# Two-layer perceiver block on one core: the mask of the first key block moves from matmuls on the identity into a stacked row, and two tables of step numbers change

## The reference, cut to what matters

```python
def xattn(query, key, value, mask, ...):        # x (2,256,256), ctx (2,4096,256), 16 heads of 16
    q = split(query @ w_q.T + b_q); k = split(key @ w_k.T + b_k); v = split(value @ w_v.T + b_v)
    scores = where(mask, -inf, (q @ k.T) / 4)   # mask (1,1,256,4096): True hides a key
    return softmax(scores) @ v  -> @ w_o.T + b_o
x = x + xattn(layernorm(x), ctx, ctx, mask, ...)
x = x + retention(layernorm(x), ...)            # 4 heads, rope, decay, gate
x = x + experts(layernorm(x), ...)              # 8 experts, gates below 0.1 dropped
```

## Time and profile before

| | us |
|---|---|
| median of 3 runs | 245.83 (245.18 to 247.62) |
| the profiled execution's own time | 246.22 |
| its span in the trace | 244.3 |
| PE busy in the span | 223.3 (91%) |
| DVE busy | 151.4 (62%) |
| ACT busy | 111.5 (46%) |
| POOL busy | 42.5 (17%) |
| mean granted PE clock | 0.988 |

### The profile page before, as it was taken

How to read it: one execution, slowest core, us unless ns; L and a number is a source line. 1 busy time by engine, 2 the same in 40 slices (tenths; PEclk the granted TensorE clock), 3 DMA queues, 4 the chain that set the end, 5 groups by cost and what they waited for, 6 DMA issues and landing times.

```text
span 244.3 us, 3831 instructions
## 1 busy us (share of the span) xinstructions
PE 223.3 (91%) x1394; PEld 122.9 (50%) x1394; DVE 151.4 (62%) x349; ACT 111.5 (46%) x237; POOL 42.5 (17%) x45
## 2 busy tenths in 40 slices
PE   8699999799799999999999898989898988899892
PEld 8368554444455645454544434535745753635340
DVE  3493789937626559696865073494457538586682
ACT  2245845557157476767677684233053051201000
POOL 6003999959000400000000000000000000000000
PEclk9999999999799999999999999999999999999997
DMA  6589678037409500550000000000000000000000
GB/s 189 198 213 321 198 183 332 4 78 179 102 13 262 163 1 3 170 179 1 3 2 3 1 0 0 1 3 0 0 0 3 0 1 1 0 0 24 23 25 25
DMA packets 15233, 17.74 MB, mean 73 GB/s; under 512 B 2573, under 2 KB 14313, under 8 KB 15209
## 3 DMA queue, kind: packets, MB, share of 16 engines
q1 hardware_dynamic: 13929, 17.11, 24.1%
q10 hardware_dynamic: 1280, 0.33, 0.7%
HBM read 9.79 MB, written 0.52 MB: 42 GB/s over the span
## 4 chain that ended last, share of the span: by engine, by line
PE 60%; DVE 18%; DMA 7%; SPq 6%; ACT 4%; issue 3%; DVEq 0%; ACTq 0%
PE bank L811 9%; PE bank L795 8%; PE bank L996 8%; PE bank L733 6%; DVE cneg L1561 6%; DMA ctxT<-in_ctxT 6%; PE bank L903 6%; PE bank L694 4%; SPq L399 4%; PE bank L976 3%; PE bank L864 3%; PE bank L681 3%; ACT prob L1245 2%; SPq L390 2%; PE bank L884 1%
## 5 line engine op out<-in xcount | busy, mean ns | idle before, releaser
L1561 DVE TENSOR_REDUCE cneg<-bank 128x1 f32<-128x896 f32 x64 | 68.0, 1087 | 32.7 <-PE bank L733 32.6
L1245 ACT ACTIVATE prob<-bank 128x512 f32<-128x512 f32 x112 | 65.5, 597 | 28.0 <-PE bank L795 19.3
L795 PE MATMUL bank<-qstack,kstack 99*128 99x256 bf16 x224 | 42.3, 274 | 1.3 <-ACT prob L1245 1.1
L733 PE MATMUL bank<-kstack,qstack 96*128 96x448 bf16 x128 | 38.5, 354 | 2.8 <-DVE cneg L1561 2.8
L811 PE MATMUL bank<-prob,vals 128*32 128x256 f32 x448 | 35.8, 391 | 0.4 <-ACT prob L1245 0.4
L795 PEld LDWEIGHTS bank<-qstack,kstack 99*128 99x128 bf16 x224 | 17.4, 97 | 24.8 <-issue 10.8
L903 PE MATMUL bank<-w_late,xnT 128*128 128x512 f32 x48 | 22.0, 595 | 0.3 <-ACT xnT L1274 0.3
L733 PEld LDWEIGHTS bank<-kstack,qstack 96*128 96x128 bf16 x128 | 12.4, 98 | 12.0 <-DVE cneg L1561 4.0
L996 PE MATMUL bank<-ctxT,xnT 128*128 128x512 f32 x32 | 17.1, 616 | 0.3 <-DVE x_in L1742 0.3
L1742 DVE SCALAR_TENSOR_TENSOR x_in<-bank,nwts,x_in 128x256 f32<-128x256 f32 x32 | 15.5, 484 | 2.5 <-PE bank L996 1.4
L996 PE MATMUL bank<-kpart,xnT 128*128 128x512 f32 x32 | 16.3, 592 | 0.0
(11 more groups left out here) (148 smaller groups left out, 277.9 us busy)
## 6 DMA issues: line engine op xcount, KB each, us to landing
kstack<-kpart SPq DMA_DIRECT2D x24, 224.0 KB, 3.6
w_late<-in_w_ret SPq DMA_DIRECT2D x1, 1536.0 KB
mask_all<-in_mask SPq DMA_DIRECT2D x2, 512.0 KB, 5.0
ctxT<-in_w_exp SPq DMA_DIRECT2D x1, 1024.0 KB
kpart<-in_w_exp SPq DMA_DIRECT2D x1, 1024.0 KB
ctxT<-in_ctxT SPq DMA_DIRECT2D x2, 448.0 KB, 6.6
ctxT<-in_ctxT SPq DMA_DIRECT2D x1, 896.0 KB, 8.8
qstack<-acc SPq DMA_DIRECT2D x12, 64.0 KB, 3.7
```

What stands on the lines that cost most here:

```text
L733: mm = pe.matmul(out, qstack[0:MROW, h, b, qt * P:(qt + 1) * P], kstack[0:MROW, b, h, half_ * HC:(half_ + 1) * HC], start=True, stop=not h ...
L795: mm = pe.matmul(out[:, hh * NQ:(hh + 1) * NQ], kstack[0:KROWS, b, h, kt * P:(kt + 1) * P], qstack[0:KROWS, h, b, :], start=(hh == 0 or no ...
L1245: act.activation(prob[:, n % PROBS, :], bank[:, S0 + jj, :], ACT.Exp).then_inc(c["prob_ready"], 1)
L1561: dve.tensor_reduce(cneg[:, st % 2, i:i + 1], bank[:, pair:pair + 2, 0:HC], AXXY, ALU.max, negate=True).then_inc(c["max_read"], 1)
```

## The change

- The mask of the first block becomes one more row of the stacks: row 96 of `kstack` holds -1e30 for hidden keys of the first block and 0 elsewhere, row 96 of `qstack` ones, and the three parts of the maximum move to rows 97 to 99. The maximum tiles contract 97 rows (before 96), the scores 100 (before 99). The matmuls L738 and L799 are gone from the fast branch.
- The rows of ones on the key side come by DMA from a small tile `edge` (4 x 896: zeros, then three rows of ones), at the end of each `stack_keys`; for n = 0 POOL fills them by a memset of 4 x 3584, and ACT issues a DMA with the mask row after making it (`first_row`). The three later memsets on POOL are gone. Ones on the query side are memset once: batch 0 by DVE at the very start, batch 1 by POOL ahead of `queries_cut(1)`.
- ACT counts per key of the first block how many queries hide it (`count_hidden`); DVE and the existing sum turn the fast branch off if any count is neither 0 nor 256.
- Stage 1's tiles go to steps `(m - 10) * 2 // 3`: steps 0 to 3 hold tiles 10, 11 / 12 / 13, 14 / 15 (before 10, 11 / 12, 13 / 14, 15 / none). So the rows of stage 1 are turned at step 5 (before 4).
- `LATER`: the keys n = 3 go to step 8 (before 5), the first values of batch 1 to step 12 (before 11).
- SP stacks the second batch right after the branch; the rows of stage 1 come after the keys n = 2, and the late weights after them.

```diff
@@ -47,7 +48,7 @@
-KROWS = MROW + 3
+KROWS = MROW + 4
@@ -83,7 +85,7 @@
         elif st == 1:
-            out.append((m - FIRST_TILES) // 2)
+            out.append((m - FIRST_TILES) * 2 // 3)
         else:
@@ -97,7 +99,7 @@
-LATER = {5: ("k", 3), 11: ("v", 0), 18: ("v", 1)}
+LATER = {8: ("k", 3), 12: ("v", 0), 18: ("v", 1)}
@@ -175,6 +178,10 @@
+    def stacked(self, n):
+        return self.at(f"k_stacked{n}", 96 if self.loop else 96 + 16)
@@ -252,8 +259,11 @@
-        hide_q0 = sb("hide_q0", [P, QT, P], BF16)
-        hide_k0 = sb("hide_k0", [P, NQ], BF16)
+        hides0 = sb("hides0", [P, NQ], BF16)
+        hidden_from = sb("hidden_from", [P, 1])
+        edge = sb("edge", [KROWS - MROW, CH], BF16)
@@ -388,6 +398,11 @@
+            def stack_edges(n, loaded):
+                b, f = divmod(n, KIN)
+                sp.dma_start(kstack[MROW:KROWS, b, f * HF:(f + 1) * HF, :], edge[:, :].unsqueeze(1).to_broadcast([KROWS - MROW, HF, CH])
+                             ).then_inc(loaded, 16)
@@ -436,6 +451,7 @@
             stack_keys(only, 1)
+            stack_edges(1, only["k_stacked1"])
             fast = is_fast(sp)
@@ -443,19 +459,21 @@
             with sp.If(fast > 0):
-                late_weights()
-                load_rows(only, 1)
                 stack_second_batch()
                 stack_keys(only, 2)
+                load_rows(only, 1)
+                stack_edges(2, only["k_stacked2"])
+                late_weights()
                 load_rows(only, 2)
                 stack_keys(only, 3)
+                stack_edges(3, only["k_stacked3"])
                 late_constants()
@@ -499,15 +521,12 @@
-            def rows_of_ones(n):
-                b, f = divmod(n, KIN)
-                rows = kstack[MROW:KROWS, b, f * HF:(f + 1) * HF, :].rearrange("r h k -> r (h k)").bitcast(F32)
-                pool.memset(rows, TWO_ONES).then_inc(s["ones_ready"], 1)
-                pool.wait_ge(s["ones_ready"], n + 1)
-            pool.wait_ge(s["const_ready"], 2)
-            rows_of_ones(0)
+            pool.memset(edge[:, :], 1.0).then_inc(s["edge_ready"], 1)
+            pool.wait_ge(s["edge_ready"], 1)
+            pool.memset(edge[0:1, :], 0.0).then_inc(s["edge_ready"], 1)
+            pool.wait_ge(s["edge_ready"], 2)
+            pool.memset(kstack[MROW:KROWS, 0, 0:HF, :].rearrange("r h k -> r (h k)").bitcast(F32), TWO_ONES).then_inc(s["ones_ready"], 1)
+            pool.wait_ge(s["ones_ready"], 1)
@@ -555,6 +574,9 @@
+            in_rows = qstack[MROW:KROWS, :, 1, :].bitcast(F32)
+            pool.memset(in_rows, TWO_ONES).then_inc(s["ones_ready"], 1)
+            pool.wait_ge(s["ones_ready"], 2)
             queries_cut(1)
@@ -592,20 +614,15 @@
                 pool.wait_ge(s["q_cut"], 3)
-                pool.wait_ge(*only.at("max_cut", 1))
-                rows_of_ones(1)
                 keys_cut(only, 2)
-                pool.wait_ge(*only.key("k_cut", 2))
-                rows_of_ones(2)
                 keys_cut(only, 3)
-                pool.wait_ge(*only.key("k_cut", 3))
-                rows_of_ones(3)
                 stream_and_bias()
@@ -714,28 +731,27 @@
                     pe.wait_ge(q_stacked[2 * b + g // 2], 96)
-                    pe.wait_ge(*c.at(f"k_stacked{2 * b + g // 2}", 96))
+                    pe.wait_ge(*c.stacked(2 * b + g // 2))
                     if c.loop:
                         settle(pe)
+                if b and g == 0 and not c.loop:
+                    pe.wait_ge(s["ones_ready"], 2)
                 if m == 0:
-                    pe.wait_ge(s["ident_ready"], 16 + 1)
                     pe.wait_ge(s["q0_taken"], 1)
...
                     else:
-                        pe.wait_ge(s["hide_first"], 2)
+                        pe.wait_ge(s["ones_ready"], 1)
+                        pe.wait_ge(s["rows_of_one"], 2)
                 pair = take_pair(c, "m", m)
...
                     out = bank[:, pair + half_, 0:HC]
-                    hides = c.loop or half_ == 0
-                    mm = pe.matmul(out, qstack[0:MROW, h, b, qt * P:(qt + 1) * P], kstack[0:MROW, b, h, half_ * HC:(half_ + 1) * HC],
-                                   start=True, stop=not hides, skip_group_check=True)
+                    mm = pe.matmul(out, qstack[0:MROW + 1, h, b, qt * P:(qt + 1) * P], kstack[0:MROW + 1, b, h, half_ * HC:(half_ + 1) * HC],
+                                   start=True, stop=not c.loop, skip_group_check=True)
                     if c.loop:
                         mm = pe.matmul(out, identb[:, :], hide_q[:, qt, half_ * HC:(half_ + 1) * HC], start=False, stop=True, skip_group_check=True)
-                    elif half_ == 0:
-                        pe.matmul(out[:, 0:P], identb[:, :], hide_q0[:, qt, :], start=False, stop=True, skip_group_check=True)
                 mm.then_inc(c["max_ready"], 1)
@@ -789,14 +806,12 @@
-                hides = c.loop or kt == 0
...
-                                   start=(hh == 0 or not hides), stop=not hides, skip_group_check=True)
-                if hides:
-                    hidden = hide_k[:, kt, :] if c.loop else hide_k0[:, :]
-                    mm = pe.matmul(out, identb[:, :], hidden.unsqueeze(1).to_broadcast([P, 2, NQ]),
+                                   start=(hh == 0 or not c.loop), stop=not c.loop, skip_group_check=True)
+                if c.loop:
+                    mm = pe.matmul(out, identb[:, :], hide_k[:, kt, :].unsqueeze(1).to_broadcast([P, 2, NQ]),
@@ -1153,10 +1169,18 @@
-            def hide_first():
+            def first_row():
...
-                act.activation(hide_k0[:, :], mask_k0[:, :], ACT.Copy, scale=HIDDEN).then_inc(s["hide_first"], 1)
+                act.wait_ge(s["edge_ready"], 2)
+                act.activation(edge[0:1, 0:P], mask_q0[0:1, 0, :], ACT.Copy, scale=HIDDEN).then_inc(s["first_row"], 1)
+                act.wait_ge(s["first_row"], 1)
+                act.wait_ge(s["ones_ready"], 1)
+                act.dma_start(kstack[MROW:MROW + 1, 0, 0:HF, :], edge[0:1, :].unsqueeze(1).to_broadcast([1, HF, CH])).then_inc(only["k_stacked0"], 16)
+            def count_hidden():
+                act.activation(hides0[:, :], mask_k0[:, :], ACT.Copy, accum_out=hidden_from[:, :]).then_inc(s["first_row"], 1)
@@ -1469,6 +1494,9 @@
+            dve.memset(mpart[:, :, :, 0, :], 1.0).then_inc(s["rows_of_one"], 1)
+            dve.memset(qstack[MROW:KROWS, :, 0, :].bitcast(F32), TWO_ONES).then_inc(s["rows_of_one"], 1)
@@ -1070,7 +1084,8 @@
-                pe.matmul(bank[0:1, OB, ODD_ALL:ODD_ALL + 2], minus[:, :], early_sums[:, :], start=True, stop=True,
+                pe.wait_ge(s["uneven"], 1)
+                pe.matmul(bank[0:1, OB, ODD_ALL:ODD_SUMS], minus[:, :], early_sums[:, :], start=True, stop=True,
```

More of the change, by code:

```diff
@@ L341, in build @@
         mask_loaded = [sem(f"mask_loaded{t}") for t in range(QT)]
-        only = Chunk({n: sem(n) for n in [*PER, *("first_k_" + n for n in ("hi", "taken", "mid", "cut"))]}, 0, False)
+        only = Chunk({n: sem(n) for n in [*(n for n in PER if n not in LOOP_ONLY), *("first_k_" + n for n in ("hi", "taken", "mid", "cut"))]}, 0, False)
         loop_sems = {n: sem(f"loop_{n}") for n in PER}
@@ L466, in _ @@
                 sp.wait_ge(s["more_ready"], 2)
+                sp.wait_ge(s["windows_added"], 1)
+                sp.wait_ge(s["edge_cleared"], 1)
+                for n in range(NB * KIN):
+                    stack_edges(n, s["edges_again"])
                 count = sp.value_load(n_windows[0:1, 0:1], min_val=1, max_val=NCH)
@@ L605, in _ @@
                 pool.wait_ge(s["q_cut"], 3)
-                rows_of_ones(1)
-                rows_of_ones(2)
-                rows_of_ones(3)
+                pool.wait_ge(*only.stacked(0))
+                pool.wait_ge(*only.stacked(1))
+                pool.memset(edge[0:1, :], 0.0).then_inc(s["edge_cleared"], 1)
+                pool.wait_ge(s["edge_cleared"], 1)
                 pool.wait_ge(s["more_ready"], 2)
@@ L1379, in _ @@
             act.wait_ge(s["odd_summed"], 1)
-            act.activation(odd_row[:, 0:ODD_ALL + 2], bank[0:1, OB, 0:ODD_ALL + 2], ACT.Copy, accum_out=any_odd[:, :]).then_inc(s["odd_counted"], 1)
+            act.activation(odd_row[:, 0:ODD_SUMS], bank[0:1, OB, 0:ODD_SUMS], ACT.Copy, accum_out=any_odd[:, :]).then_inc(s["odd_counted"], 1)
             act.wait_ge(s["odd_counted"], 1)
@@ L1495, in _ @@
             first_layernorm(1)
+            dve.wait_ge(s["first_row"], 2)
+            dve.scalar_tensor_tensor(early_sums[:, 2:3], hidden_from[:, :], float(NQ), hidden_from[:, :], ALU.subtract, ALU.mult).then_inc(s["uneven"], 1)
             def start_again():
@@ L1506, in start_again @@
                 for n in range(KIN):
-                    dve.wait_ge(*only.at(f"k_stacked{n}", 96))
+                    dve.wait_ge(*only.stacked(n))
                 for n in range(NB * KIN):
```

37 lines of the change are left out of this document (20 added, 17 removed).

## The result

| | before | after |
|---|---|---|
| median of the runs (lowest to highest) | 246.23 us (245.18 to 247.62), 4 runs | 239.97 us (239.15 to 240.14), 4 runs |
| profiled execution, span | 246.22, 244.3 | 239.15, 237.2 |
| mean granted clock in it | 0.988 | 0.995 |

The changed kernel takes 0.9736 of the time, 95% interval 0.9685 to 0.9788: 6.3 us less, 240.0 where 240.3 was forecast. A second comparison gave 0.9828 (0.9777 to 0.9879; 241.06 and 245.56). The two intervals overlap only from 0.9777 to 0.9788; what differs between them is shown further on, with the clock.

What follows compares the result with a forecast made beforehand. PE, busy 91%, was taken as the bound, with DVE setting the pace in the early steps. Terms 0 + 0 + 0.2 + 4.5 gave 4.7 with the clock's fall, 6.3 without; forecast 240.3 us, range 237.9 to 243.3.

Steps and rivals of the forecast that it cites:

- The price of the masks: Steps of kt = 0 and tiles on PE: 0.06 per query mask, 0.22 per key mask, start to start.
- Start: Up to 38.55, before step 1: the added memsets, small activation and DMA are hidden by waits; 0 us.
- the cover: Start, on POOL: the added memset of 1.8 fits into its idle 2.25 before the scan, 0.4 left.
- Steps 0 to 8: From 38.55 to step 9: 0 us, DVE sets the pace and a 1.2 wait for stage 1's rows eats the rest.
- Steps 9 to 12: Gain 0.2: masks 0.3, wait -0.1 (1.65 for DVE at tile 26, was 1.54), and the clock at half chance.
- Step 13 to the end: PE stays the bound: gain 4.5, between 3.8 and 4.8, from tile masks 2.2, key masks 2.2 and 0.4, less 0.3.
- the clock's fall: Steps 9 to 12, whether the clock falls again: half chance each; total gain 4.7 with it, 6.3 without.
- All waits go: Rival: stage 1's rows land in time, the key cut hurts at most 0.4, no clock fall: 237.1; chance 0.10.
- The early waits grow: Rival: stage 1's rows land late behind key stacks, clock falls behind both waits: 243.3, up to 244.5; chance 0.19.
- The 97th row: Rival: a fourth group of 32 rows makes each tile matmul 0.06 longer: 247.0; chance 0.03.
- the general branch: Rival: the first block's mask is judged uneven, the branch with loops runs, far above the time before; chance 0.02.

Runs made afterwards that it cites:

- masks_off: The kernel before without its two kinds of mask matmuls, memsets and order kept: 240.78 us, ratio 0.9774.
- old_order: The changed kernel with the order of before (last keys step 5, late values step 11, two tiles per early step), run twice: 238.86 and 237.69 us.
- memsets_first: The kernel before with POOL's three late memsets of ones moved to the start: 247.36 us, ratio 1.0012.
- cut_after: The changed kernel, POOL's cut of the last keys waiting until DVE has cut the maxima of stage 2: 238.75 us, ratio 0.9691.
- all_three: The changed kernel, POOL's last key cut and bias sum held behind DVE's cuts of stages 2 and 3, stage 1's rows turned a step sooner: 237.76 us, ratio 0.9701.
- after_again: The changed kernel unaltered, timed once more in the second comparison: 241.06 us, ratio 0.9828.

## Why the prediction came out right

**The price of the masks: right.** 0.06 and 0.22, start to start. Each later stage is 12.12 - 11.25 = 0.87 shorter, forecast 8 x 0.06 + 2 x 0.22 = 0.92, and masks_off without any new order or edge has the same pitch.

**Start: the cover held.** Tile 0 and step 1 come 0.8 and 0.7 earlier. Tile 0 follows the first keys on PE, and these the first context transfer: 7.94 before, 6.54 after, 7.74 to 7.76 with tile 0 at 22.70 and 22.73 in the two runs of old_order, which has the same start as the changed kernel. So the 0.8 is mostly when that transfer landed. The ten profiles with the new edges have tile 0 between 21.86 and 22.73, the three of the old kernel with its memset in place 22.90, 24.00 and 24.30 (the last two with the clock down at the start); whether the change has a share in that stays open. One reading of mine was wrong: POOL's memset of ones is not longer (3.08 for four rows, as for three before), but it starts at 3.39 instead of 1.73, behind the two memsets of `edge`. So it runs until 6.47 and held a TENSOR_SCALAR of the first layer norm for 1.32 instead of 0.17, which I had not counted; the keys on PE covered it. memsets_first shows what becomes of it without the cover.

**Steps 0 to 8: right.** Forecast 0, measured 19.21 before and 18.85 after from step 1 to step 9. DVE's reads set the pace, and the rows of stage 1 cost 1.01 for 1.2.

**Steps 9 to 12: the mechanism right.** DVE's CAST and subtraction took 0.96 and 0.90, and PE waited 1.41 for 1.65 before tile 26; cut_after took the cause away and the wait with it. I gave the clock half a chance to fall; in the profiled execution it did not, and 13.96 became 11.48, a gain of 2.5 where the sum had 1.8 for that case.

**Step 13 to the end: the term that failed.** I had 4.5, between 3.8 and 4.8; measured are 76.94 - 73.48 = 3.5. The step was "only the tile two behind a cut comes within 0.1, for which I take off 0.3 in all": it looked at DVE and PE alone. I had asked what a faster PE makes collide for the keys, not for POOL's sum of the bias, which starts when SP's queue has let its row through. It now meets the cut of stage 3 and costs 0.8 at tile 34 (all_three: 15.16 to 14.33 between two turns). The remaining 0.2, and the 0.3 that I had already taken off, went in small pieces that no run takes apart (a later stage gained 0.87 for 0.92).

**The total** of the profiled execution, 7.1, is my 6.3 without the clock's fall, plus 0.7 at the start, plus 0.4 and 0.7 in the steps 0 to 8 and 9 to 12, less 1.0 from step 13 on. That 240.3 was hit to 0.3 is partly such cancelling.

**The clock explains most of why two comparisons differ.** Each run has its mean granted clock and span. The kernel before at 0.996, five runs: 241.5 to 242.1, mean 241.8. The changed kernel at 0.995 and 0.996, four runs: 237.2 to 238.3, mean 238.0. The difference at an equal clock is 3.8; at 1.000 there are one run of before (242.2) and two of the changed kernel (238.0 and 237.5), 4.4. That is about my 4.7 less the 0.8 of the bias. The rest of the 6.3 (and of the 4.5 in the second comparison) goes with how often the clock fell: before went down to 0.982 and 246.3, the changed kernel to 0.990 and 240.1. The two profiles of the changed kernel show one such fall. Up to the last turn of outputs they agree within 0.15 (141.69 and 141.83); then after_again has a granted clock of 0.59 from 180 to 184, in the retention, and takes 97.2 to the end where the first took 95.5.

**The rivals.** "All waits go" was priced at 237.1; the kernels in which the waits for the rows and for DVE's cuts do go measure 237.4 and 236.5. "The early waits grow" did not come, though all_three shows how near it was: its mechanism, the queues shared with the key stacks, is real and made 2.0 of 1.0 as soon as the rows were issued sooner. The 97th row and the general branch fell.

## What to carry to other kernels

Price a matmul by the start of the next one, and then ask for each idle engine what it will now run into: two of the three new waits came from POOL work that had stood beside none of DVE's cuts before. Work on an engine that holds up its neighbour is best placed by a wait on the moment when the neighbour is done, which gave 3.0 in the old kernel for one line; moved to where its own engine idles, it cost as much as it saved. A small transfer that somebody waits for is issued ahead of large ones, and turning its source out earlier is worth nothing while they stand before it.
